# A two-layer transformer forward on one core: the order in which five hand-overs between engines are written

## What is computed

```
x = LN(x + attn0(x))   # 16 heads, half of q,k plain, half rotary; causal; out @ Wo.T
x = LN(x + moe(x))     # sigmoid gate, top 2 of 8 experts (hidden 256), plus a shared expert
x = LN(x + attn1(x))   # one head over 512, biased q,k,v, rotary per 128, not causal, @ o_w.T
x = LN(x + mlp(x))     # silu(x Wg) * (x Wu), keep 2 of each 4 by size, @ Wd (hidden 2048)
```

## Time and profile before

| | us |
|---|---|
| median of three runs | 2268.38 |
| the profiled execution's own time | 2271.96 |
| its span in the profile | 2270.2 |
| TensorE busy | 2172.7 (96%) |
| VectorE busy | 1191.6 (52%) |
| ScalarE busy | 753.1 (33%) |
| GpSimd busy | 670.4 (30%) |
| mean granted TensorE clock | 0.983 |

### The profile page before, as it was taken

How to read it: one execution, slowest core, us unless ns; L and a number is a source line. 1 busy time by engine, 2 the same in 40 slices (tenths; PEclk the granted TensorE clock), 3 DMA queues, 4 the chain that set the end, 5 groups by cost and what they waited for, 6 DMA issues and landing times. The chain is left out here.

```text
span 2270.2 us, 27500 instructions
## 1 busy us (share of the span) xinstructions
PE 2172.7 (96%) x10148; PEld 1497.2 (66%) x10148; DVE 1191.6 (52%) x2324; ACT 753.1 (33%) x1351; POOL 670.4 (30%) x458
## 2 busy tenths in 40 slices
PE   8999999999999899999979999999998999999997
PEld 6876555555553644444457778888877888888885
DVE  6877677676661643222247542322236546554666
ACT  3325555555556332111134321111223221211223
POOL 5345555555556105332223250000003021211200
PEclk9989999999999999999999999999999999999999
DMA  5478245343300625555534460000101010100001
GB/s 198 176 204 199 81 118 132 95 89 71 71 15 21 247 79 211 136 115 90 85 105 142 149 231 20 28 19 19 47 1 56 1 38 19 38 18 18 19 19 56
DMA packets 104605, 197.27 MB, mean 87 GB/s; under 512 B 10385, under 2 KB 27665, under 8 KB 103057
## 3 DMA queue, kind: packets, MB, share of 16 engines
q1 hardware_dynamic: 92064, 162.78, 24.5%
q0 software_dynamic: 11408, 29.69, 5.8%
q10 hardware_dynamic: 1008, 3.15, 0.4%
HBM read 123.82 MB, written 71.75 MB: 86 GB/s over the span
## 5 line engine op out<-in xcount | busy, mean ns | idle before, releaser
L684 ACT ACTIVATE a_probs<-a_stb 128x512 f32<-128x512 f32 (+3 forms) x640 | 309.8, 535 | 240.6 <-PE a_stb L825 126.4
L650 POOL TENSOR_TENSOR a_probs<-a_probs 128x1024 f32<-128x1024 f32 (+3 forms) x158 | 278.4, 1775 | 247.5 <-PE a_avb L837 233.6
L722 DVE TENSOR_REDUCE a_mparts<-a_sbank 128x1 f32<-128x512 f32 x384 | 240.0, 683 | 86.3 <-PE a_sbank L799 86.1
L2207 POOL CAST m_wh<-wst 128x1024 fp32r<-128x1024 f32 x24 | 26.7, 1112 | 720.8 <-POOLq L1510 368.9
L57 PE MATMUL m_gu<-hi,m_wh 128*128 128x512 f32 x512 | 200.5, 392 | 4.7 <-DVE m_h L2282 2.8
L58 PE MATMUL m_gu<-lo,m_wh 128*128 128x512 f32 x512 | 199.9, 390 | 0.0
L59 PE MATMUL m_gu<-hi,m_wl 128*128 128x512 f32 x512 | 199.8, 390 | 0.0
L837 PE MATMUL a_avb<-a_probs,V 128*32 128x512 f32 (+3 forms) x1280 | 151.6, 546 | 0.7 <-ACT a_probs L684 0.7
L2282 DVE TENSOR_TENSOR m_h<-m_sg,m_gu 128x512 f32<-128x512 f32 x64 | 44.0, 688 | 193.8 <-ACT m_sg L2237 193.5
L727 DVE CUSTOM_DVE_ANT_0 a_junk<-a_sbank,hidden 128x128 bf16<-128x128 f32 (+3 forms) x256 | 113.4, 488 | 55.9 <-PE a_sbank L799 54.4
L799 PE MATMUL a_sbank<-hi,q 96*128 96x512 f32 (+3 forms) x304 | 119.4, 418 | 7.6 <-DVE a_mparts L722 4.2
(11 more groups left out here) (284 smaller groups left out, 4761.3 us busy)
## 6 DMA issues: line engine op xcount, KB each, us to landing
qk<-v_hl SPq DMA_DIRECT2D x32, 512.0 KB, 3.0
hi<-qk SPq DMA_DIRECT2D x60, 256.0 KB, 5.1
lo<-qk SPq DMA_DIRECT2D x60, 256.0 KB, 5.3
wst<-in_w_mlp SPq DMA_DIRECT2D x24, 512.0 KB, 3.5
q<-qk SPq DMA_DIRECT2D x42, 256.0 KB, 5.8
xs<-a_zeros POOLq DMA_DIRECT2D x39, 264.0 KB, 2.8
X<-xs SPq DMA_DIRECT2D x39, 264.0 KB, 2.7
v<-vhl SPq DMA_DIRECT2D x16, 512.0 KB, 5.1
```

The costliest lines, as they stand in the source:

```text
L650: nc.gpsimd.tensor_tensor(probs[:, i % PSLOTS, hs, w0:], probs[:, i % PSLOTS, hs, w0:], probs[:, (i + 1) % PSLOTS, hs, w0:], ALU.add)\
L684: nc.scalar.activation(probs[:, i % PSLOTS, h, w0:], stb[:, k % 3, w0:], ACT.Exp, scale=SCALE0)\
L722: nc.vector.reduce_max(to, sbank[:, b, :], AX).then_inc(s["unit_max"], 1)
```

## The change

Only the order of work, and which engine does one split, are changed; all arithmetic on the data is the same.

1. layer0_qkv: weight piece 3 is split by ScalarE and VectorE, piece 4 ahead of the first cosines, piece 5 behind them; a high cast stands one event later on ScalarE, a low part one step later on VectorE; the last chunk has its four qk groups first.
2. layer0_project: "ranks" stands behind ("w", 3, 0).
3. The last two scatters, not one, are issued in layer1_attention; there all five fusions come first, the v bias is loaded first, and ScalarE has a root without use ahead of the last fusion.
4. Layer-1 projections: roots, statistics and applies of the next chunk's tiles are spread over the first three pieces, statistics between sines and sums.
5. layer1_mlp: the product of ("up", c = 1, r = 0) stands behind the first hl of the first pick.

```diff
@@ layer0_qkv, events @@
-            return ev + [("qk", c, 3), ("v", c, 1), ("v", c, 2), ("v", c, 3)]
+            return [("qk", c, j) for j in range(NG)] + [("v", c, t) for t in range(TC)]
@@ GpSimd @@
             split(2)
-            split(3)
+            split(4)
             for what, c, j in events:
                 if what == "qk":
                     cosines(c, j)
-                    if c == 0 and j < 2:
-                        split(4 + j)
+                    if c == 0 and j == 0:
+                        split(5)
@@ ScalarE @@
-            last_qk = events.index(("qk", NC - 1, NG - 1))
-            acts = events[:last_qk + 3] + [("high", NC - 1, NG - 1)] + events[last_qk + 3:]
+            acts = []
+            for i, ev in enumerate(events):
+                acts.append(ev)
+                if i > 0 and events[i - 1][0] == "qk":
+                    acts.append(("high", *events[i - 1][1:]))
...
                             act.dma_start(wst[:, i % 3, :], piece_in(i)).then_inc(wload[i % 3], 16)
+                            if i == 4:
+                                split(3)
...
-                if what == "high" or (what == "qk" and k < NC * NG - 1):
+                elif what == "high":
@@ VectorE @@
-            for what, c, j in events:
+            steps = []
+            for i, (what, c, j) in enumerate(events):
+                swapped = [ev for ev in events[:i] if ev[0] == "qk"][-1:] if what != "v" else []
+                held = [("low", *ev[1:]) for ev in swapped if ("low", *ev[1:]) not in steps]
+                if what == "qk":
+                    steps += [("swap", c, j)] + held + [("sum", c, j)]
+                elif what == "x":
+                    steps += [("x", c, j)] + held
+            steps.append(("low", NC - 1, NG - 1))
+            for what, c, j in steps:
...
                         split(1)
+                        split(3)
@@ TensorE @@
-                        pe.wait_ge(s["wlo_d" if j < 2 else "wlo_p"], 3 if j < 2 else j + 1)
+                        pe.wait_ge(s["wlo_d" if j < 2 else "wlo_p"], 3 if j < 2 else j)
...
-                        pe.wait_ge(s["wlo_p"], 2)
+                        pe.wait_ge(s["wlo_p"], 1)
+                        pe.wait_ge(s["wlo_d"], 4)
@@ layer0_project @@
-            ev += [("ranks", 0, -1)] * before + [("b", 1, 0), ("w", 3, 0)]
+            ev += [("b", 1, 0), ("w", 3, 0)] + [("ranks", 0, -1)] * before
...
                         act.wait_ge(s["gt_ok"], g + 1)
+                        if not opening:
+                            act.wait_ge(s["sm_ok"], g)
@@ layer0_experts, GpSimd; LATE = 2 @@
-            for j in range(NR - 1):
+            for j in range(NR - LATE):
@@ layer1_attention, SP @@
+            sp.dma_start(bvr[:], v_bias).then_inc(s["bias_in"], 16)
...
-            sp.dma_start(bvr[:], v_bias).then_inc(s["bias_in"], 16)
@@ GpSimd @@
-            pool.wait_ge(added, 16 * (NR - 1))
-            nc.gpsimd.indirect_dma_start(acc_dram[:, :], bass.IndirectOffsetOnAxis(ap=last_to, axis=0), last_rows, None,
-                                         compute_op=ALU.add).then_inc(added, 16)
+            for i in range(LATE):
+                pool.wait_ge(added, 16 * (NR - LATE + i))
+                nc.gpsimd.indirect_dma_start(acc_dram[:, :], bass.IndirectOffsetOnAxis(ap=last_to[i], axis=0), last_rows[i],
+                                             None, compute_op=ALU.add).then_inc(added, 16)
@@ ScalarE @@
+            fuse(0)
             act.wait_ge(s["bias_in"], 16)
             nc.scalar.activation(bvh, bvr[:].unsqueeze(2).broadcast_to([P, ND, P]), ACT.Copy).then_inc(s["bvh_ok"], 1)
-            fuse(0)
-            weight(1, 0)
-            weight(1, 1)
             fuse(1)
-            weight(1, 2)
-            weight(1, 3)
+            fuse(2)
+            for d in range(ND):
+                weight(1, d)
+            fuse(3)
+            nc.scalar.activation(nrm.std[:, NT - 1:NT], nrm.eps[:], ACT.Sqrt)
+            fuse(ND)
             root(0)
...
+                out(i)
+                out(i + 1)
                 if c + 1 < NC:
                     root(n)
-                    root(n + 1)
+                out(i + 2)
+                if c + 1 < NC:
                     apply(n)
-                    apply(n + 1)
-                out(i)
-                out(i + 1)
-                out(i + 2)
                 high(p)
                 out(i + 3)
                 if c + 1 < NC:
+                    root(n + 1)
                     root(n + 2)
                 out(i + 4)
+                if c + 1 < NC:
+                    apply(n + 1)
+                    apply(n + 2)
                 high(p + 1)
@@ VectorE @@
+                for t, tiles in enumerate(((n,), (n + 1, n + 2), (n + 3,))):
+                    sines(p + t)
+                    for k in tiles if c + 1 < NC else ():
+                        stats(k)
+                    sums(p + t)
+                    for k in tiles if c + 1 < NC else ():
+                        apply(k)
+                    low(p + t)
@@ TensorE @@
-            for j in range(3):
+            for j in range(ND + 1):
                 fuse(j)
             turn(0)
-            fuse(3)
             turn(1)
-            fuse(ND)
@@ layer1_mlp, VectorE @@
                     elif what == "up":
+                        if (c, r) == (1, 0) and is_first(q):
+                            continue
...
+                            if c == 0 and r == 0 and is_first(q):
+                                dve.wait_ge(s["hl_ok"], 1)
+                                dve.wait_ge(s["sg_ok"], 5)
+                                tt(h[:, 0, :], sg[:], gu[:, 0, 1, :], ALU.mult).then_inc(s["h_ok"], 1)
```

More of the change, by code:

```diff
@@ L275, in split @@
                 nc.gpsimd.tensor_copy(piece_of(i, wqh, wvh), wst[:, i % 3, :]).then_inc(s["whi_p"], 1)
-                pool.wait_ge(s["whi_p"], i - 1)
+                pool.wait_ge(s["whi_p"], (2, 4, 5).index(i) + 1)
                 nc.gpsimd.tensor_tensor(piece_of(i, wql, wvl), wst[:, i % 3, :], f32(piece_of(i, wqh, wvh)),
@@ L293, in split @@
             def split(i):
-                act.wait_ge(wload[i], 16)
-                nc.scalar.activation(piece_of(i, wqh, wvh), wst[:, i, :], ACT.Copy).then_inc(s["whi_a"], 1)
+                act.wait_ge(wload[i % 3], 16 * (i // 3 + 1))
+                nc.scalar.activation(piece_of(i, wqh, wvh), wst[:, i % 3, :], ACT.Copy).then_inc(s["whi_a"], 1)
             def split_half(a):
@@ L348, in split @@
             def split(i):
-                dve.wait_ge(s["whi_a"], i + 2)
-                tt(piece_of(i, wql, wvl), wst[:, i, :], f32(piece_of(i, wqh, wvh)), ALU.subtract)\
+                dve.wait_ge(s["whi_a"], (0, 1, 3).index(i) + 2)
+                tt(piece_of(i, wql, wvl), wst[:, i % 3, :], f32(piece_of(i, wqh, wvh)), ALU.subtract)\
                     .then_inc(s["wlo_d"], 1)
@@ L368, in _ @@
                         split(1)
-                elif what == "qk":
+                        split(3)
+                elif what == "swap":
                     dve.wait_ge(s["qkf_ok"], k + 1)
@@ L373, in _ @@
                     nc.vector.stream_shuffle(rotated[:], qkf[:, k % 2], SWAP).then_inc(s["rot_ok"], 1)
+                elif what == "sum":
                     if j == 0:
@@ L381, in _ @@
                     tt(t1[:, k % 2], t1[:, k % 2], rotated[:], ALU.add).then_inc(s["sum_ok"], 1)
+                elif what == "low":
                     dve.wait_ge(s["hi_ok"], k + 1)
@@ L914 @@
 AHEAD = 2
+LATE = 2
 def shared_up(nc, w0, xt, ab, c, j):
@@ L1496, in _ @@
             down(NR - 1, old)
-    return s["added"], y[:, (NR - 1) % 2, :], to[:, NR - 1:NR]
+    late = range(NR - LATE, NR)
+    return s["added"], [y[:, j % 2, :] for j in late], [to[:, j:j + 1] for j in late]
 READY = 12
@@ L1721, in _ @@
                 weight(0, d)
+            fuse(0)
             act.wait_ge(s["bias_in"], 16)
             nc.scalar.activation(bvh, bvr[:].unsqueeze(2).broadcast_to([P, ND, P]), ACT.Copy).then_inc(s["bvh_ok"], 1)
-            fuse(0)
-            weight(1, 0)
-            weight(1, 1)
             fuse(1)
-            weight(1, 2)
-            weight(1, 3)
+            fuse(2)
[4 more added lines that the diff above has]
+            fuse(ND)
             root(0)
-            fuse(2)
             apply(0)
             root(1)
+            apply(1)
             turn(0)
-            apply(1)
-            fuse(3)
             root(2)
+            apply(2)
             turn(1)
-            apply(2)
-            fuse(ND)
             root(3)
@@ L1765, in _ @@
                 if c + 1 < NC:
-                    apply(n + 2)
+                    root(n + 3)
                 out(i + 6)
                 if c + 1 < NC:
-                    root(n + 3)
+                    apply(n + 3)
                 high(p + 2)
@@ L1772, in _ @@
                 if c + 1 < NC:
-                    apply(n + 3)
                     turn(n)
@@ L1878, in _ @@
```

(35 more changed lines are left out.)

## The result

| | before | after |
|---|---|---|
| median, us | 2269.53 (19 runs) | 2265.70 (19 runs) |
| lowest to highest | 2267.77 to 2282.41 | 2259.82 to 2272.31 |
| ratio | | 0.9978, 95% interval 0.9968 to 0.9988 |
| profiled execution | 2271.96 | 2264.27 |
| its span | 2270.2 | 2262.5 |

The change is a little faster: 5.0 us by the ratio (2.7 to 7.3), 7.7 in the two profiled executions, where 12.2 were forecast. (The medians alone differ by 3.8 us.) 2265.7 lies above the range of 2247 to 2263, and above the 2263.9 that the prediction set as the bound of "faster".

A forecast was written before the change was run, and what follows sets the result against it. TensorE was taken as the bound, busy 2172.7 of 2270.2 us (96%). Terms 0.6 + 1.5 + 5.1 + 2.0 + 3.0 = 12.2 us, off the median of 2268.38, gave 2256; range 2247 to 2263.

The forecast's parts named there:

- A: layer0_qkv, new split of weight pieces and order of casts: +0.6 us won, from −0.6 to +2.5.
- B: layer0_project, ranks behind tile 3's chain: +1.5 us won, from 0 to +4.
- C: Experts to layer 1, two late scatters with all fusions first: +5.1 us won, from −2 to +6.5.
- D: Layer-1 projections, roots, statistics and applies spread over the pieces: +2.0 us won, from −0.5 to +4.
- E: The MLP's opening, product behind the first hl part: +3.0 us won, from 1.2 to 3.0.
- it needs the copy of group 1, which ended at 44.17 and now ends near 43: layer0_qkv: value group 3 is late next, with a wait of some 3 us at about 40.
- Gain 0.5, twice: layer0_project: otl, made behind the ranks, done at 777.8 instead of 778.33, so 0.5 us won two times.
- some half clock: layer0_project: some lost time at half clock also won, within the +1.5 us; no size of its own.
- The drain: layer0_project: about 1.38 us per ScalarE table switch beside the 1.28 load; with it B would be about −1.3.
- rival 3: Whole kernel: stalls only move; A, B and D give 0, C and E 8.1 us, so 2260; chance 0.15.
- Rivals 1 and 4: 1: experts' end doesn't follow the last scatter, 2261 to 2263, chance 0.13; 4: layer-1 projection loops slower, 2276, chance 0.03.
- Rival 2: Behind the hand-off to layer0_attention the clock comes back earlier: −4 us, 2252; chance 0.15.

The follow-up runs named there:

- e11: Kernel before with the new order of fusions and DMAs in layer 1's opening, but only one late scatter as before; ratio 1.0003.
- e12: Kernel before with the last two scatters issued in layer 1's stage, fusions, turns and bias DMA in their old order; ratio 0.9993.
- e3: Kernel before with only the new places of the high casts and low parts in layer0_qkv; ratio 1.0008.
- e9: Kernel before with C and E alone; ratio 0.9968.
- e4: Changed kernel with ScalarE's copy of value group 1 ahead of rotary group 2's high cast, and the last chunk's second value copy ahead of its last high; ratio 0.9976.
- e5: Changed kernel with only the weight pieces of layer0_qkv split as before; ratio 0.9966, median 2261.05 us.
- e7: Changed kernel with the ranks ahead of tile 3 again in layer0_project; ratio 0.9983.
- e8: Changed kernel with the layer-1 projection loops in their old order; ratio 0.9982.
- e1: Changed kernel with the whole first stage, layer0_qkv, as before; ratio 0.9956, median 2261.41 us.
- e6: Kernel before with C alone: two late scatters, all fusions first, v bias first; ratio 0.9989.

## Why the prediction was wrong

By the marks the forecast of 12.2 missed 2.8 us in A, 1.5 in B, 0.8 in C, 1.3 in D and 0.2 in E, and 2.0 came by luck from the clock between scores and MLP. That makes 7.6 of the 7.7.

**A, forecast +0.6 (−0.6 to +2.5), measured −2.2.** The step that failed is "it needs the copy of group 1, which ended at 44.17 and now ends near 43". The shape was right: the wait at 23 us shrank to 0.4, and one came up at 40, for that copy. Its size was 5.32 us, not 3. Rows of the chain that ends in the copy, first of the kernel before, then of the changed one:

```profile
18.50 3.39 POOL L269 TENSOR_TENSOR X<-X,v_cs 128x1024 f32<-128x1024 f32 x1
...
28.51 2.05 DVE L377 TENSOR_TENSOR v_rotated<-v_rotated,v_cs 128x1024 f32<-128x1024 f32 x1
...
39.28 1.23 DVE L381 TENSOR_TENSOR X<-X,v_rotated 128x1024 f32<-128x1024 f32 x1
...
40.54 1.06 ACT L335 ACTIVATE v_hl<-X 128x1024 fp32r<-128x1024 f32 x1 [5.50 <-DVE X L381]
```

```profile
23.16 2.40 POOL L269 TENSOR_TENSOR X<-X,v_cs 128x1024 f32<-128x1024 f32 x1
...
29.86 3.39 POOL L269 TENSOR_TENSOR X<-X,v_cs 128x1024 f32<-128x1024 f32 x1
...
30.91 3.42 DVE L393 TENSOR_TENSOR v_rotated<-v_rotated,v_cs 128x1024 f32<-128x1024 f32 x1
...
42.34 1.23 DVE L397 TENSOR_TENSOR X<-X,v_rotated 128x1024 f32<-128x1024 f32 x1
...
43.59 1.06 ACT L340 ACTIVATE v_hl<-X 128x1024 fp32r<-128x1024 f32 x1 [3.92 <-DVE X L397]
44.56 0.58 ACT L343 ACTIVATE V<-v_vb 128x512 f32<-128x512 f32 x1
```

Cosines 0 end at 25.56 instead of 21.89, 3.7 us later (forecast: about 3). VectorE's sum for the third rotary group is still 3.1 later, so is ScalarE's high cast of it, and behind that cast the copy now stands. It ends at 45.14, 1.0 later than before. The prediction said that all on VectorE comes later, and then let the copy end earlier: with its own 3 us in that sum the copy comes out at 45.1. TensorE was there 4.3 us earlier than before (39.87 against 44.21), so 4.3 won and 1.0 lost make the wait of 5.3. Behind it stands a stretch of 3.4 us at half clock (45.0 to 48.4), which the sum put at nothing. It is as long as the one that left at 26, and value group 3 takes 1.4 us more by it. So the rotary group behind starts at 49.52 instead of 47.11: 2.4 us of loss.

A part of the lateness is that piece 4 landed 0.9 us later than reckoned (its cast starts at 19.36). Contention adds little: VectorE's product with the sines takes 3.42 us at 30.91, issued while GpSimd multiplies by the cosines, and ends 1.1 us behind GpSimd's end. That fits what the page "SBUF — State Buffer" of the Trainium skill says under "Who interferes with whom": an operation of VectorE with two SBUF inputs contends with a GpSimd operation that reads SBUF, and one of them is held until the other is done. But the kernel before has such overlaps too (2.05 at 28.51), and from the first rotary group's sum to the second's VectorE takes 8.7 us in the changed kernel and 8.6 before.

**The last chunk.** The hand-off gap went from 3.1 to 1.2 us, since TensorE and no longer VectorE ends last. But TensorE ends 4.1 us later (149.41 against 145.32), where 0.4 to 2.3 was forecast: 2.4 us come from the first chunk, and 1.45 are the wait for a copy behind a high cast. VectorE's last low part ends 0.6 us earlier (147.07 against 147.63), not 2.

**B, forecast +1.5, measured 0.** The mechanism was right to 0.1 us: ranks end at 779.27 (with the 2.1 us of shift taken off 777.2), otl behind them, TensorE's wait is 3.06. The step that failed is to count "Gain 0.5, twice" and "some half clock" as gains of the end: 0.4 us was there at the end of the stage (95.96 us instead of 96.38) and went by the end of the experts. The stretches at half clock in the two stages are as long as before (13.6 us).

The drain that the page "ScalarE: Activation LUTs" of the Trainium skill gives in its section "What ACT_TABLE_LOAD costs" did not come: in the changed kernel the load starts at 775.08 and the sigmoid at 776.37, again 0.01 us behind its end.

**C, forecast +5.1, measured +4.3.** The hand-off (4.9 against 4.8) and the chain (rows read 12.9 behind the start against 12.6) were right. The term that was mis-sized is the wait for tile 0, 4.40 us and not 2.6. The fusions ran at full clock and ended 13.9 us behind the start, where the forecast had 15.2 (1159.5 less 1144.3), and the transposes of tile 0 came at 18.3 instead of 17.8. Behind the wait the next 6.8 us run at half clock, which the sum did not hold. The prediction took the two edits as one; e11 and e12 show that it does take both.

**D, forecast +2.0, measured 0.7 in these two profiles and nothing over all of them.** The loops did shrink, but by 0.7 and 1.9 us and not by 2.1 each: value groups follow each other by 39.3 and 38.4 us (1209.09, 1248.39, 1286.78) instead of 40.0 and 40.3, and the first chunk took 2.4 us more, not 1.8. TensorE's two waits of 3.3 us became 1.5 and 1.2 in each loop, before turns and values, and the wait for the store of v is the same. Also here the stall moved on.

**E, forecast +3.0, measured +2.8**, with the 1.5 us idle (1.56) and the clock of 1.0. Right. More than half of it is the fall of the clock behind the long wait, and e11 has that wait without the fall.

So rival 3 was the nearest (A, B and D nothing; 2260 by it), and it had 0.15; even it had no loss in A. I gave the forecast 0.54 for the sum of five terms of which three (A, B and D) rested on one mechanism: a removed wait leaves most of its length won, although the displaced work then stands ahead of another consumer. Rivals 1 and 4 are excluded by the marks. Rival 2 didn't come: 23.9 us at half clock behind the hand-off instead of 27.3, and the attention stage took 591.6 us in both. The chance of 0.91 for faster is right by the direction alone: by its own bound of 0.2% the ratio (0.9978) is just beyond, but its interval lies on both sides of 0.998.

## What to carry to other kernels

Before a wait is costed as won, follow the work that was put back down to the next thing that TensorE needs, engine by engine, and carry the delay through every step: in three of five places the removed wait came back under another name, once larger. A hand-off that waits for a DMA chain pays more with other work to put beneath the chain: by the marks the two edits gave 1.7 and 0 us apart and 4.2 together. And a shorter idle time can be worth more than the difference in length if it keeps the clock up: part E's 1.2 us brought 2.8, in an execution where the clock would have fallen.

## What the runs showed of the hardware

The scatter between executions of the same kernel (2259.8 to 2272.3) goes with the granted clock: over the 19 runs of the changed kernel the mean clock is between 0.978 and 0.988, and the longest run has the lowest, the shortest the highest. Where it comes from can be seen only in profiled executions. Behind the hand-off to layer0_attention TensorE is busy and yet at 1.2 GHz, in all fourteen. A stretch of 24 to 28 us is usual there. The two longest profiled executions have more of it, e3 38 us and e9 48:

```profile
150.00:200.00 50.00, 48.49 (x186) 32.31 (x186) 32.79 (x131) 13.75 (x32) 23.54 (x19) 0.53 0.78 177
```

In the changed kernel the clock was 1.00 through the idle time of the hand-off and fell 3.6 us later (at 154.2), under matmuls that keep PE busy by the profile:

```profile
150.00:154.00 4.00, 3.16 (x12) 1.96 (x12) 3.05 (x19) 0.05 (x1) 3.31 (x3) 1.00 0.67 260
154.00:178.00 24.00, 22.24 (x64) 14.88 (x65) 17.29 (x77) 4.88 (x10) 13.70 (x10) 0.50 0.70 150
```

With 1.2 us of idle time ahead it fell 1.9 to 4.0 us behind the first matmul (changed kernel, e4, e5, e7, e8), with 3.1 us between 1.0 ahead of it (e1) and 2.1 behind (e6). So making that idle time shorter did not keep the clock up. What makes it fall was not tried. The stretch is the longest at half clock in this kernel: 24 us.
